# One straight schedule over all chunks: the last expert halves of a chunk placed between the steps of the next preparation

## What is computed

```
def mamba(x):                      # L0_attn
    h = rmsnorm(x) ; xi, z = split(h @ W_in.T)              # 512 inner channels each
    xi = silu(causal_conv4(xi) + b)
    dt, B, C = split(xi @ W_x.T) ; delta = softplus(dt @ W_dt.T + b)
    for t in tokens:               # the recurrence, 16 states a channel
        s = s * exp(delta[t] * A) + delta[t] * B[t] * xi[t] ; y[t] = s @ C[t]
    return ((y + xi * D) * silu(z)) @ W_out.T + x
x = layernorm(x + mamba(x))
x = layernorm(x + cross_attention(x, ctx))   # 8 heads, 2*64 keys, expert 3 of the weights, then a relu layer
x = layernorm(x + moe(x))                    # 8 experts, top 2 by weight, all computed densely, + 1 shared
```

## Time and profile before

| what | value |
|---|---|
| median of 3 runs (lowest, highest) | 1206.05 us (1203.5, 1207.94) |
| profiled execution: its own time | 1208.32 us |
| span from first to last instruction in it | 1206.2 us |
| busy share of the span: PE, DVE, ACT, POOL | 76%, 73%, 44%, 44% |
| mean granted clock of TensorE (share of 2.4 GHz) | 0.812 |
| the chain that ended last: PE, issue, DVE, POOL | 35%, 25%, 23%, 10% |

### The profile page before, as it was taken

How to read it: one execution, slowest core, us unless ns; L and a number is a source line. 1 busy time by engine, 2 the same in 40 slices (tenths; PEclk the granted TensorE clock), 3 DMA queues, 4 the chain that set the end, 5 groups by cost and what they waited for, 6 DMA issues and landing times.

```text
span 1206.2 us, 13806 instructions
## 1 busy us (share of the span) xinstructions
PE 919.9 (76%) x3960; PEld 693.9 (58%) x3960; DVE 877.0 (73%) x1255; ACT 530.1 (44%) x995; POOL 528.2 (44%) x311
## 2 busy tenths in 40 slices
PE   4935559658679998568689999578679994767996
PEld 2534446246468785256478775266468782544885
DVE  1599996498999966599989964689889964212333
ACT  3534342734446534645446625554445522322442
POOL 1256640254357850453457830443467822001452
PEclk9855558868769999878669999778689997665998
DMA  5110100102023311111023311101023303000431
GB/s 196 37 35 35 53 1 35 71 18 78 20 69 108 89 51 55 71 36 62 18 73 121 91 33 55 71 36 62 18 80 118 92 27 113 0 1 13 119 114 35
DMA packets 38254, 72.61 MB, mean 60 GB/s; under 512 B 3871, under 2 KB 12712, under 8 KB 38174
## 3 DMA queue, kind: packets, MB, share of 16 engines
q1 hardware_dynamic: 38174, 71.65, 18.5%
HBM read 65.14 MB, written 2.30 MB: 56 GB/s over the span
## 4 chain that ended last, share of the span: by engine, by line
PE 35%; issue 25%; DVE 23%; POOL 10%; ACT 5%; DVEq 1%; POOLq 0%; DMA 0%; ACTq 0%; SPq 0%
PE ps L883 8%; DVE hs L1067 8%; POOL dbu L532 7%; PE ps L960 5%; PE ps L739 4%; DVE yacc L1119 4%; PE ps L857 4%; PE ps L812 2%; DVE work L1235 2%; PE ps L818 2%; POOL work L564 2%; PE ps L797 2%; PE ps L790 1%; PE ps L902 1%; DVE work L1214 1%
## 5 line engine op out<-in xcount | busy, mean ns | idle before, releaser
L532 POOL TENSOR_TENSOR dbu<-v,bbc 128x1024 f32<-128x1024 f32 x128 | 308.8, 2417 | 249.2 <-DVE v L1053 129.4
L1067 DVE TENSOR_TENSOR_SCAN hs<-ps,carry,dbu 128x512 f32<-128x512 f32 x256 | 313.3, 1265 | 7.9 <-ACT ps L635 5.8
L635 ACT ACTIVATE ps<-delta,neg_a 128x512 f32<-128x512 f32 x256 | 175.3, 692 | 244.9 <-DVE hs L1067 244.7
L739 PE MATMUL ps<-ident,hs 128*128 128x128 f32 x1024 | 186.2, 340 | 90.0 <-DVE yacc L1119 74.5
L739 PEld LDWEIGHTS ps<-ident,hs 128*128 128x128 f32 x1024 | 156.8, 179 | 120.2 <-DVE hs L1067 73.3
L1119 DVE SCALAR_TENSOR_TENSOR yacc<-ps,ctok,yacc 128x512 f32<-128x512 f32 x240 | 167.2, 737 | 1.2 <-PE ps L739 1.0
L556 POOL TENSOR_TENSOR w_lo<-w13s,w_hi 128x512 fp32r<-128x512 f32 x72 | 93.0, 1293 | 134.2 <-ACT w_hi L714 132.4
L960 PE MATMUL ps<-w2s,work 128*128 128x256 f32 x576 | 136.8, 381 | 0.3
L883 PE MATMUL ps<-x_hi,w_hi 128*128 128x512 f32 x288 | 109.2, 462 | 9.4 <-DVE work L1241 9.1
L960 PEld LDWEIGHTS ps<-w2s,work 128*128 128x128 f32 x576 | 106.3, 191 | 15.0 <-DVE work L1241 1.5
L1235 DVE SCALAR_TENSOR_TENSOR work<-work 128x512 f32<-128x512 f32 x72 | 81.5, 1132 | 45.9 <-POOL work L564 45.0
(11 more groups left out here) (162 smaller groups left out, 1233.1 us busy)
## 6 DMA issues: line engine op xcount, KB each, us to landing
w13s<-in_w SPq DMA_DIRECT2D x72, 256.0 KB, 2.9
bbc<-brow_dram SPq DMA_DIRECT2D x32, 512.0 KB, 3.9
w2s<-in_w SPq DMA_DIRECT2D x36, 256.0 KB, 2.7
cbc<-comb_dram SPq DMA_DIRECT2D x32, 256.0 KB, 3.5
work<-work SPq DMA_DIRECT2D x16, 256.0 KB, 2.3
xn<-in_x SPq DMA_DIRECT2D x5, 512.0 KB, 5.0
xt<-in_x SPq DMA_DIRECT2D x4, 512.0 KB, 3.8
rope<-in_rope_q SPq DMA_DIRECT2D x4, 512.0 KB, 4.2
```

The lines of the kernel that those rows point to most:

```text
L532: pool.tensor_tensor(dbu[:, i % DRING, :, :], v[:, 2 * h:2 * h + 2, :], bbc[:, n // 2 % 2, n % 2, :].rearrange("p (o t) -> p o t", o=1) .t ...
L635: act.activation(ps[:, unit % 2, :], delta[:, q, :], ACT.Exp, scale=neg_a[:, q * NS + m:q * NS + m + 1]).then_inc(da_done.sem, 1)
L739: last = pe.transpose(ps[:, bank, t * P:(t + 1) * P], src(t), ident[:, :])
L1067: dve.tensor_tensor_scan(hs[:, m % 2, q, 0:TC], ps[:, unit % 2, :], dbu[:, n % DRING, q % 2, :], carry[:, m, q:q + 1], ALU.mult, ALU.add). ...
```

## The change

The hardware loop goes: `schedule()` now returns one list over all chunks with the chunk numbers in it, and every engine's program is laid out straight. The 41 ticks of a chunk are dealt out anew. Ticks 0 to 34 stand beside the 35 steps of the next chunk's recurrence (tick t beside step t; before, tick t beside step t - 2). Ticks 35 to 40 are carried over to the preparation of the recurrence after that: 35 after pre 1, 36 after pre 2, 37 and 38 after pre 3, 39 after pre 4, 40 after pre 6. Since banks 6 and 7 then still hold expert sums, pre 4 uses bank 0 and the transposes of pre 5 bank 3, with a wait ahead of the fourth `wdt` product.

```diff
-    steps = [("setup", 0), ("pre", 1), ("post", 3), ("post", 4), ("pre", 2), ("post", 5), ("pre", 3)] + tick(0)
-    steps += [("pre", 4), ("pre", 5), ("early", 1), ("pre", 6), ("late", 1), ("setup", 1)]
...
-        t = PRE_TICKS + s
-        steps += [("early", t), ("sum", s), ("mid", t), ("scan", s), ("late", t)]
...
-    for k, t in enumerate(range(PRE_TICKS + SCAN_TICKS, T_OUT + 1)):
-        steps += [("post", k)] if k < 3 else []
-        steps += tick(t)
+    for i in range(CHUNKS + 1):
+        new, mixed, last = i < CHUNKS, i - 1, i - 2
+        left = list(range(SCAN_TICKS, T_OUT + 1))
...
+        steps += mixer(i, "pre", 1)
+        steps += second(last, left[0])
+        steps += mixer(mixed, "post", 3) + mixer(mixed, "post", 4)
+        steps += mixer(i, "pre", 2)
+        steps += second(last, left[1])
+        steps += mixer(mixed, "post", 5)
+        steps += mixer(i, "pre", 3)
+        steps += second(last, left[2]) + second(last, left[3])
+        steps += mixer(i, "pre", 4)
+        steps += second(last, left[4])
+        steps += mixer(i, "pre", 5)
+        steps += mixer(i, "pre", 6)
+        steps += second(last, left[5])
...
+        for s in range(SCAN_TICKS):
+            steps += second(mixed, s, ("early",)) + mixer(i, "sum", s) + second(mixed, s, ("mid",))
+            steps += mixer(i, "scan", s) + second(mixed, s, ("late",))
...
+        for n in range(3):
+            steps += mixer(i, "post", n)
+    for t in left:
+        steps += second(CHUNKS - 1, t)
...
-            body(0, True, False)
-            with eng.Fori(1, CHUNKS, 1) as i:
-                body(i, False, False)
-            body(CHUNKS, False, True)
+            for stream, chunk, kind, step in SCHEDULE:
+                if stream == "mixer":
+                    mixer(chunk, kind, step)
+                else:
+                    second(chunk, step, kind)
...
-                    act.activation(rows_t[:, :], ps[:, 6, :], ACT.Copy).then_inc(rows_done.sem, 1)
+                    act.activation(rows_t[:, :], ps[:, 0, :], ACT.Copy).then_inc(rows_done.sem, 1)
...
-                    transposes(7, lambda t: rows_t[:, t * P:(t + 1) * P], NT, ct_ps)
+                    transposes(3, lambda t: rows_t[:, t * P:(t + 1) * P], NT, ct_ps)
                     for q in range(Q):
                         pe.wait_ge(*sz_done.at(j, q + 1))
+                        if q == 3:
+                            pe.wait_ge(*ctok_done.at(j, 1))
```

More of the change, by code:

```diff
@@ new lines, in schedule, with mixer, second @@
+    for i in range(CHUNKS + 1):
+        new, mixed, last = i < CHUNKS, i - 1, i - 2
+        left = list(range(SCAN_TICKS, T_OUT + 1))
+        def mixer(chunk, *what):
+            return [("mixer", chunk, *what)] if 0 <= chunk < CHUNKS else []
+        def second(chunk, t, parts=("early", "mid", "late")):
+            return [("second", chunk, p, t) for p in parts] if 0 <= chunk < CHUNKS else []
+        if i == 0:
+            for n in range(4):
+                steps += mixer(0, "fetch", n)
+            steps += mixer(0, "setup", 0)
+        steps += mixer(i, "pre", 1)
[11 more added lines that the diff above has]
+        steps += second(last, left[5])
+        if i == 0:
+            steps += mixer(0, "setup", 1)
+        for s in range(SCAN_TICKS):
+            steps += second(mixed, s, ("early",)) + mixer(i, "sum", s) + second(mixed, s, ("mid",))
+            steps += mixer(i, "scan", s) + second(mixed, s, ("late",))
+            if new and SCAN_TICKS - 12 <= s < SCAN_TICKS - 8:
+                steps.append(("mixer", i + 1, "fetch", s - SCAN_TICKS + 12))
+        for n in range(3):
+            steps += mixer(i, "post", n)
@@ L789, in mixer @@
                         pe.wait_ge(*u_done.at(j, q + 1))
[L790 removed]
+                        last = pe.matmul(ps[:, 0, :], wxp[:, q, :], u[:, q, :], start=(q == 0), stop=(q == Q - 1))
                     last.then_inc(xp_ps.sem, 1)
```

29 lines of the change are left out of this document (2 added, 27 removed).

## The result

The changed kernel takes **1237.82 us** (median of 4 runs, 1236.15 to 1242.37), the kernel before in the same comparison 1206.99 us (4 runs, 1203.5 to 1211.59). The ratio is **1.0271, 95% interval 1.0244 to 1.0298**: slower by 30.8 us, where 21.7 us were forecast. The profiled execution took 1238.42 us, with a span of 1236.6 us.

What follows compares the result with a forecast made beforehand. PE bounds the boundaries, DVE the recurrences. Boundary 1 -1.8, recurrences -3.6, boundaries 2 and 3 +11.2 and +7.6, last boundary +8.3 sum to +21.7 us: 1206.05 becomes 1227.8, range 1212 to 1241.

Steps and rivals of the forecast that it cites:

- rival (A): PE idles after pre 5, so each recurrence's query product runs at 1.2 GHz: +19 us, 1247, half of it 1237; chance 0.15.
- my sum: Whole kernel: all stage terms added, +21.7 us to 1227.8 us, own range 1219 to 1237; chance 0.62.
- the signs named: New profile: first scans about 71 us behind post 0, `u,wxp` not waiting for `u`, 29 to 30 us first to fifth scan.
- Boundaries 2 and 3: From T, start of post 0, to first scan after recurrences 1 and 2: T+70.8, +11.2 and +7.6 us.
- PE's pile: At boundaries 2 and 3, tick 37 and tick 38's b and o delay `u,wxp` to T+42.2; 0.5 of 7.6 us hidden.
- The output norm: Tick 40 between v and the first scan: one uncovered chain DVE, POOL, DVE, ACT of 6.75 us.
- Boundary 1: Post 0 to first scan after recurrence 0: no carried ticks, loses the query copies that held ACT, -1.8 us.
- Recurrences: Recurrences 1 to 3: ticks 0 and 1 in the first steps, 29.6 against 30.8 us, -1.2 each, -3.6 in all.
- The rotation: End of the query chain, 18.5 us as in the last chunk; DVE waits for it until S+22.8, S being the first scan.
- Last boundary: Post 0 of the last chunk to its query product: PE's row without a gap 27.3, then tick 40 and copies, +8.3 us.
- rival C: Straight code is quicker by itself: at 0.3 us saved a step of the looped recurrences, 1196 us; chance 0.08.
- rival B: Products of ticks 37 to 39 fall into unseen PE waits: 17.8 us less, 1210, no change that can be told; chance 0.10.

Runs made afterwards that it cites:

- experiment 5: Changed kernel with only the first of three terms in the carried gating products of halves 16 and 17, chunks 0 to 2: 1238.58 us, ratio 1.0256.
- experiment 2: Changed kernel with POOL's third input product of recurrences 2 and 3 held back until DVE's shift of tick 40: 1237.64 us, ratio 1.0271.
- Experiment 3: Changed kernel with tick 40 split: additions and statistics behind pre 5, power, shift, scalings and store behind step 1 of the recurrence: 1213.54 us, ratio 1.0055.
- experiment 8: Kernel before, laid out straight in its own order, with ACT's query copies moved behind the first scans: 1213.39 us, ratio 1.0063.
- Experiment 6: Changed kernel with POOL's power for the norm of x1 asked for at post 5 instead of post 4, behind tick 36: 1238.68 us, ratio 1.0285.
- experiment 1: Kernel before in its old order, with only the hardware loop laid out straight: 1203.21 us against 1206.88, ratio 0.9974 (0.9942 to 1.0006).
- experiment 9: Changed kernel with carried ticks 35 to 40 put back ahead of the preparation, behind post 0, 1, 2: 1221.20 us, ratio 1.0122.
- experiment 4: Changed kernel with tick 0 and tick 1's query product, not its copies, ahead of step 0 of each recurrence: 1240.3 us, ratio 1.0288.
- experiment 7: Changed kernel with tick 40 split, its late part behind step 5, and POOL's power for x1 behind tick 36: 1221.49 us, ratio 1.0128.
- the filling: 31 further products, read by nothing, in PE's waits of the last chunk: old order laid out straight 1197.54 us, changed kernel 1234.72 us.

## Why the prediction was right, step by step

The sign and most of the mechanism were right, and 1237.8 lies in the range; the sum was 9 us short. By the time alone it is also what half of rival (A) would give (1237), and just above my sum's own range (to 1237); it is the stages that tell them apart. Of the signs named, the first scans at T+71.6 and T+72.5, `u,wxp` without a wait for `u` and the additions ahead of step 3 came; first to fifth scan took 32.7 to 33.0 us instead of 29 to 30. In the prediction's own terms:

- **Boundaries 2 and 3** (+11.2, +7.6; measured +11.9, +9.3). Two parts of this were off. *PE's pile was right as a time and too dear as a price.* I had `u,wxp` wait until T+42.2 behind ticks 37 and 38, and it started at T+41.6. But I had its silus allow it at T+35.1, so that 7.1 us of the pile stood open. They allowed it at T+37.9 (experiment 5, where PE is early enough), so 3.7 us were open, and taking 3.1 us of PE's work away gave only 1.0 back. The convolution, which I took to last as before, took 10.42 us for its eleven operations where it took 7.38:

```profile
460.18 10.42 DVE L1113 SCALAR_TENSOR_TENSOR u<-hs,vec,u 128x512 f32<-128x512 f32 x11 [0.91 <-ACT u L654]
...
465.35 3.38 POOL L572 TENSOR_TENSOR work<-work,cbc 128x512 f32<-128x512 f32 x2
```

  POOL's products of the carried tick run beside it now. Three of the eleven operations, those beside the rows of POOL, take 1.75 to 1.77 us each, the other eight 0.74 to 0.75 as before. v then ended at T+60.7, not 61.9. *The output norm was sized too small*: 6.75 us, measured from the first addition to the last scaling 8.85, of which 2.1 are the shift beside POOL (experiment 2). The two errors, v 1.2 us early and what follows it 2.0 us longer, partly cancelled in boundary 2, which is luck. Experiment 3 shows the whole price of the norm, 10.4 us a boundary with what follows.
- **Boundary 1** (-1.8; -3.7). That it loses the query copies is right in kind; experiment 8 takes only them out and shortens boundaries 2 and 3 by 2.3 and 2.5 us. The other 1 to 2 us are within what the same instructions differ by from run to run (51.13 and 53.59).
- **Recurrences** (-1.2 each; +0.6, +2.0, +1.1). The start of the query product (S+4.3) and its length (9.21, forecast 9.18) were right, and rival (A), a product at half clock throughout, fell. The rotation was mis-sized: its additions took 6.64 us instead of 4.49, with POOL busy beside both, and the `top` of step 3 1.71 us, which in the last chunk takes 0.17. I had written that in the last chunk nothing else ran. But POOL's rotation product ran beside the first of the two additions there, which took 3.36 us, and only the second, with nothing beside it, took 1.21. The price for the recurrence stood in the same trace, 6.63 us in step 0. The first four steps took 3.0 to 3.4 us more than forecast (32.65 to 33.01 against 29.6), which covers the 1.8 to 3.2 us by which a recurrence is off.
- **Last boundary** (+8.3; +12.5). PE's row (27.3) was counted without a gap, and POOL's order was not looked at: the power for x1 holds up the low half of a17 and the products of halves 15 and 16. Experiment 6 gives 4.9 us back by that edit alone, more than the 4.2 missing.
- **Straight code** (rival C). It does no more than 0.6% for this kernel. The Trainium skill (Runtime: NRT & Kernel Launch, Instruction fetch mechanics) says that kernels do better fully unrolled; experiment 1 shows 0.26%, with an interval that includes no change.
- **The carried products hide** (rival B, 0.10). In part it was true. Against the old order without query copies (57.44, experiment 8), boundary 2 with all of them carried and the norm split (61.10, experiment 3) is 3.7 us longer, and two more ticks in a row ahead of the preparation (69.22 and 65.88, experiment 9) make 9 to 12, in an execution above its median. I had held it against (B) that PE was busy 51.26 of 59.61 us, and had not counted that later silus give cover by themselves.

Open stays how much of the gain of experiments 4, 6 and 7 went to the granted clock and how much to waits behind moved instructions: only the last chunk was filled, the recurrences were not.

## What to carry to other kernels

When work of one stream is laid between the steps of another, look at its cheap end first: not the products, which fill waits, but the short serial chain over three or four engines (statistics, power, shift, scaling), which in a row with the next stage's first operations costs its full latency. Split it, so that no engine that the next stage needs has to wait in it. And take the price of an operation of DVE from a place in the trace where POOL does what it will do beside it later. Give a help that has nothing to do with the change, here the filling, to both orders before they are compared.
